# A Gated-DeltaNet loop: the next step's key projection set between the halves of the fourth level, and the expert's down product drained ahead of that level's copy

## What is computed

```
mixed = silu(causal_conv4(x @ w_qkv));  q, k, v = split(mixed);  z = x @ w_z
q, k = l2norm(q) / sqrt(128), l2norm(k)
for each token:  S = S * exp(g);  S = S + k (v - k.S) * beta;  o = q.S
out = rmsnorm(o * silu(z)) @ w_out
experts:  y[e] = (silu(buf[e] @ w_gate[e]) * (buf[e] @ w_up[e])) @ w_down[e]
```

## Time and profile before

| | |
|---|---|
| median of 3 runs | 3094.16 us (3086.99 to 3102.05) |
| the profiled execution's own time | 3097.86 us |
| its span | 3096.1 us |
| mean granted clock of TensorE | 0.963 |
| busy | PE 89%, PEld 74%, DVE 77%, ACT 57%, POOL 40% |
| loop over heads | from 122 to 2690 us |

### The profile page before, as it was taken

The page is one execution under the profiler, slowest core; times in us unless marked ns, Lnnn a source line. Parts: engine busy times, 40 slices in busy tenths (PEclk is TensorE's granted clock), DMA queues, the critical chain, the costliest instruction groups (busy, mean ns, idle before and its releaser), DMA issues. The chain is left out here.

```text
span 3096.1 us, 129193 instructions
## 1 busy us (share of the span) xinstructions
PE 2761.4 (89%) x52495; PEld 2287.1 (74%) x52496; DVE 2385.2 (77%) x5142; ACT 1765.9 (57%) x5625; POOL 1236.7 (40%) x1120
## 2 busy tenths in 40 slices
PE   2599989898999999999999999999999999967888
PEld 1477777777787878787878787878788888744555
DVE  7577787777877777777887878777778787638996
ACT  1366666666666666666666666666666666521111
POOL 4555555655333333333333333333333333335620
PEclk8799999999999999999999999999999999988999
DMA  4211111101111111111110111111111111163311
GB/s 170 73 52 55 42 41 31 31 27 29 44 30 42 30 44 30 44 30 44 30 44 30 44 30 37 29 37 34 39 34 41 34 41 34 34 228 98 115 63 41
DMA packets 94202, 155.58 MB, mean 50 GB/s; under 512 B 17238, under 2 KB 61829, under 8 KB 92403
## 3 DMA queue, kind: packets, MB, share of 16 engines
q1 hardware_dynamic: 69779, 112.45, 12.2%
q0 software_dynamic: 12288, 24.19, 2.5%
q10 hardware_dynamic: 11520, 10.49, 1.0%
HBM read 115.18 MB, written 41.29 MB: 51 GB/s over the span
## 5 line engine op out<-in xcount | busy, mean ns | idle before, releaser
L1278 DVE SCALAR_TENSOR_TENSOR p_y<-p_xr,p_cw,p_y 128x512 f32<-128x512 f32 x768 | 673.4, 885 | 44.3 <-ACT p_y L1027 23.8
L1085 ACT ACTIVATE p_Xs<-p_psI 128x256 f32<-128x256 f32 (+1 forms) x386 | 160.3, 415 | 523.0 <-PE p_psI L762 451.0
L714 PE MATMUL p_psF<-xnS,p_w_hl 128*128 128x512 f32 x1536 | 433.4, 419 | 21.1 <-PEq L586 21.1
L1504 POOL TENSOR_TENSOR p_E<-p_E,p_sj 128x512 f32<-128x512 f32 x128 | 131.8, 1050 | 744.2 <-DVE p_sj L1305 744.2
L714 PEld LDWEIGHTS p_psF<-xnS,p_w_hl 128*128 128x128 f32 x1536 | 278.0, 195 | 74.6 <-issue 21.7
L1323 DVE TENSOR_TENSOR p_ATP<-p_psF,p_E 128x512 f32<-128x512 f32 x256 | 166.5, 687 | 180.6 <-PE p_psF L749 171.6
L1512 POOL TENSOR_TENSOR p_M<-p_ATc,p_masks 128x512 f32<-128x512 f32 x128 | 170.4, 1336 | 308.4 <-ACT p_ATc L1065 308.4
L771 PE MATMUL p_psI<-p_Xs,p_DTc 32*32 32x32 f32 x16384 | 213.6, 196 | 66.6 <-issue 64.6
L762 PEld LDWEIGHTS p_psI<-p_Dc,p_M 32*32 32x32 f32 x16384 | 174.4, 107 | 130.9 <-issue 122.8
L771 PEld LDWEIGHTS p_psI<-p_Xs,p_DTc 32*32 32x32 f32 x16384 | 177.0, 107 | 121.0 <-issue 106.1
L762 PE MATMUL p_psI<-p_Dc,p_M 32*32 32x32 f32 x16384 | 205.5, 195 | 60.0 <-DVE p_DTc L1341 35.2
(11 more groups left out here) (328 smaller groups left out, 6541.1 us busy)
## 6 DMA issues: line engine op xcount, KB each, us to landing
p_ab<-decays SPq DMA_DIRECT2D x64, 512.0 KB, 5.3
p_w_raw<-in_w_in SPq DMA_DIRECT2D x17, 768.0 KB
expert_out<-p_ye ACTq DMA_DIRECT2D x80, 128.0 KB, 2.2
p_wgu<-in_w_gu SPq DMA_DIRECT2D x56, 176.0 KB
expert_in<-p_zero SPq DMA_DIRECT2D x16, 512.0 KB, 9.7
p_xe<-expert_in SPq DMA_DIRECT2D x56, 128.0 KB
p_wd<-in_w_down SPq DMA_DIRECT2D x56, 88.0 KB
p_wout<-in_w_out SPq DMA_DIRECT2D x16, 256.0 KB
```

The source lines that it names most:

```text
L714: m = pe.matmul(b4(psF[f % 2][:, :]), w_hl[:, wp, kt, ty * P:(ty + 1) * P], xnS[:, xp, kt, :].rearrange("p (b t) -> p b t", b=B)[:, :, c * ...
L1085: act.activation(dst, src, ACT.Copy).then_inc(s["xs" if l < 5 else "join_xs"], 1)
L1278: m = dve.scalar_tensor_tensor(y[:, ty, :, :], xr[:, ty, :, tap:tap + P], cw[:, ty, tap:tap + 1], y[:, ty, :, :], ALU.mult, ALU.add)
```

## The change

TensorE: the key projection of a step moves out of that step and into the one before, between the two halves of level 4, behind the turn of the outputs. The first is made ahead of the loop, and the last step has none. At the end of a head it projects the next head's keys, and waits for its weights there. ScalarE: the copy of the down product (L1135) goes ahead of the copy of level 4's first half.

```diff
             def step(kh, c):
 
-                project(kh, c, 0)
                 project(kh, c, 1)
                 expert(kh, c, EX_IN)
...
                 project_z(kh, c, (3,))
                 level_x(kh, c, 4)
                 turn_out(kh, c - 1)
+                if c < NC - 1:
+                    project(kh, c + 1, 0)
+                elif kh < HK - 1:
+                    project(kh + 1, 0, 0)
                 level_y(kh, c, 4)
 
+            project(0, 0, 0)
             for kh in range(HK):
                 for c in range(NC):
                     step(kh, c)
...
                 expert(kh, c, EX_UP)
                 out_squares(kh, c - 1, 1)
                 inverse_copy(kh, c, 3)
+                expert(kh, c, EX_DOWN)
                 inverse_copy(kh, c, 4)
-                expert(kh, c, EX_DOWN)
                 out_turned(kh, c - 1, 0)
                 store_expert(kh, c)
                 out_turned(kh, c - 1, 1)
```

## The result

The changed kernel takes 3108.38 us (median, 3100.44 to 3119.51) against 3092.76 us before in the same comparison: a ratio of 1.0055, 95% interval 1.0042 to 1.0067. It is slower by 0.55%, just beyond what was called the bound of no change; the forecast was 5 us and it is 16. A second comparison at the end gave 1.0063 (1.0040 to 1.0086). The profiled execution took 3106.19 us, its span is 3104.3 us.

The account below looks back on a forecast made before the run. TensorE was taken to bound the loop, losing time to issue stalls and waits. Terms -11 - 1.5 + 13 - 4.5 + 9.6 = +5.6 us, taken as 5, gave 3099 us; range 3072 to 3122 us.

Parts of the forecast that it names:

- The case that was given the largest chance: The study's own forecast: a loss of 5 us, 3099 us, within 3082 to 3110 us, chance 0.53.
- (a): Key projection, 1.51 us, goes before level 4's second half: TensorE's work unchanged, its slot free, no wait: 0.
- (b): Down product's drain, 0.38 us on ScalarE, goes ahead of level 4's copy, where ScalarE idles: costs 0.
- (c): Issue stalls in level 4's second half: each shortened by 1.44 us; of 24.3 us some 0.9 us stay.
- Rival 2: Issue stalls are no block fetches and stay, nothing pays for the later second half: 3116 to 3125 us, chance 0.12.
- (d): Level 4's second half ends 1.51 us later: net -11 us at chunks 2 and 3, -1.5 chunk 0, +13 chunk 1.
- The turn of chunk 1: Keys' turn (L739) in chunk 1: 1.26 us later in 13 heads, 0.69 in 3: 18.5 us, taken as +13.
- The clock in chunk 1: TensorE at half clock after chunk 1's longer wait: 6 of 16 heads, +9.6 us; bounds none or all (26 us).
- The gains: Fewer stalls at chunks 2 and 3 (-11 us) and chunk 0 (-1.5), fewer half-clock stretches after level 4's stalls (-4.5).
- the -4.5 us for the clock: Four half-clock stretches behind level 4's stalls, some 1.6 us each, go, partly where VectorE covers them: 4 x 1.1 us.
- Rival 3: Clock falls at every chunk 1, 26 us in place of 9.6: +22 us, 3116 us, chance 0.16.
- Rival 1: Chain behind level 4 has more room, chunk 1's keys' turn not later: about -24 us, 3070 us, chance 0.18.

## Why the prediction was right, and where it wasn't

The case that was given the largest chance came about, a small loss as the rest of larger terms of both signs, and the time lies in the range; but the loss was 16 us, not 5, and past the 0.5%, which had been given 0.27.

**What held.** (a) and (b): the projection finds its slot, the new order on ScalarE costs nothing (0.9992). (c): in level 4's second half three stalls of 0.2 to 0.4 us, 0.9 us together, are left where 24.3 us were, and 0.9 us was the forecast; the sum at L771 fell by 26.4 us where some 20 were forecast. That the stalls are block ends was argued with 254 instructions between two of them, and is now shown by the shift. Rival 2, by which they would stay, falls, and what the Trainium skill, "Runtime: NRT & Kernel Launch", says in "Instruction fetch mechanics" of a fetch that is mostly hidden does not hold in this kernel's runs of small matmuls: 57 to 65 us of stalls at L771 alone where nothing is moved. (d), chunk 1: the turn was forecast 6.13 us after the second half's end and comes 6.16 us after it; the wait was forecast at 1.9 us and is 2.04. Chunks 2 and 3: 3.2 us of wait forecast in some 20 boundaries, 4.3 us in 14 measured.

**What failed in size.** *The turn of chunk 1* was forecast 13 us later in sum, and comes 15 us later. The wait itself grew by more, 20.3 us with chunk 1 alone moved (13.4 to 33.7), the 18.5 us of the forecast; the cut from there to 13 was about right, and the 5 us between wait and turn are TensorE getting there earlier. *The clock in chunk 1* was put at 6 heads and 9.6 us, and this term was too small: it was 6 to 9 heads in the four executions with the move, and 14 us behind the turn. It rested on a misreading: I had the half clock follow in about half of the stalls of 1.4 us or more, but in the trace of the kernel before, 10 of the 12 at L771 have such a stretch beginning between 0.9 us ahead of their end and 1.6 us behind it.

*The gains.* Forecast for the other chunks and the vanished stretches at half clock: -11 - 1.5 - 4.5 = -17 us; measured -9 to -10 by the ratio, and -13 by the length of the steps, all of it in chunks 2 and 3. I had said that L897's wait would be about as before; it rose by 4.9 us (10.6 to 15.5), all of it at chunk 0, where a stall taken away just makes TensorE wait for the keys' copy behind the table load. And the -4.5 us for the clock came on top, with 1.1 of 1.6 us taken for each of four stretches, though at those places VectorE is late.

By the steps, then, chunk 1 cost 29 us instead of 22.6, and the rest brought 13 instead of 17: 16 instead of 5. Rival 3, the slower one, has the right mechanism at half strength: 6 to 9 of 16 heads, not 16. Rival 1 falls: ScalarE's chain has no room; it got room by a change of its own (the diagonals later), which took 0.5 us a head off the wait at chunk 1.

## What to carry to other kernels

Work that is set ahead of a dependency pays with the whole slack behind it: before moving a block of 1.5 us between two halves, look at each kind of iteration for who starts on the second half and how late that engine already is; here three of four had 1.4 to 1.6 us of cover and one had 0.1. When one iteration differs, move the block only where the cover is (0.9971 against 1.0081 for the move everywhere, on one chip). And when an engine is given its data earlier, look at the order on the engines behind it: what was a free order while the keys came late (diagonals ahead of the queries' copy) set the chain once they came early.

## What the runs showed of the hardware

The places of the long issue stalls are a matter of the program alone: in separate executions, and with another order on ScalarE, they come after the same matmul of the same step (after 59 and after 60 of 64 in both, for instance), only their length differs, 1.31 and 1.03 us, 1.31 and 1.58 us. In a run of small matmuls 64 instructions ahead of the loop shift each by 32 matmuls, in all 14 places that can be compared from the 15th step on. On one of the chips, short idle times of another kind came on top in the first 16 steps.

A wait of some 2 us between short pieces of work was followed by a stretch at 1.2 GHz in 31 of 64 cases (the turn of chunk 1 in four executions on the faster chips). Waits of 1.0 to 1.3 us at the same place were in 1 of 13. That is no bound for other places: with the whole output projection ahead of the turn, a wait of 1.17 us stood a little later, and the clock fell in 11 of 16. Four matmuls of no use in the wait of 2 us took all the stretches away, and brought 0.3%.
